# Attention products placed unit by unit instead of slot by slot, and one group of transposes put one slot later

## The reference, cut to what matters

```python
q1, q2 = (q[:, :, :, 0], q[:, :, :, 1])
k1, k2 = (k[:, :, :, 0], k[:, :, :, 1])
attn1 = causal_attn(q1, k1, vcat, scale)
attn2 = causal_attn(q2, k2, vcat, scale)
attn = attn1 - lambda_full * attn2
rms = jnp.sqrt(jnp.mean(attn * attn, axis=-1, keepdims=True) + EPS)
attn = attn / rms * rms_w
attn = attn * (1.0 - LAMBDA_INIT)
x = _layernorm(x + attn.reshape(B, T, H * 2 * HD) @ Wo, axis=-1)
x = _layernorm(x + _L0_ffn_ref(x, router_w, router_b, w1, w2), axis=-1)
```

## Time and profile before

| | us |
|---|---|
| median of 3 runs | 610.83 |
| the runs | 608.61, 611.09, 610.83 |
| span of the profiled execution | 609.5 |
| PE busy | 566.8 |
| DVE busy | 502.4 |
| ACT busy | 427.9 |
| POOL busy | 333.7 |

### The profile page before, as it was taken

One profiled execution on the slowest core, in us unless ns is written; L12 is line 12 of the kernel. 1 busy time (PEld: TensorE's weight loads), 2 busy tenths in 40 slices (PEclk: granted clock), 3 DMA queues, 4 the chain that ended last, 5 costly groups with the idle time before them and its releaser, 6 DMA issues.

```text
span 609.5 us, 30827 instructions
## 1 busy us (share of the span) xinstructions
PE 566.8 (93%) x12925; PEld 339.9 (56%) x12925; DVE 502.4 (82%) x1250; ACT 427.9 (70%) x903; POOL 333.7 (55%) x569
## 2 busy tenths in 40 slices
PE   5499999999999999999999999999999899999992
PEld 1245454555554555455455445545555588899992
DVE  4477898998999899899989989999994878866673
ACT  4004788998888898889888878989789635344441
POOL 5322033773577397737757773943564215765584
PEclk9555799999999999999999999999899999999997
DMA  3603313321331332134123323411102882888510
GB/s 113 182 6 110 100 36 80 108 61 33 100 106 42 96 97 79 50 87 119 35 67 85 109 58 79 112 43 52 51 8 81 275 300 67 274 284 278 189 55 22
DMA packets 44083, 62.85 MB, mean 103 GB/s; under 512 B 13436, under 2 KB 35196, under 8 KB 43800
## 3 DMA queue, kind: packets, MB, share of 16 engines
q1 hardware_dynamic: 38888, 54.31, 30.5%
q0 software_dynamic: 2416, 5.08, 2.3%
q10 hardware_dynamic: 2640, 1.48, 0.9%
HBM read 42.79 MB, written 21.65 MB: 106 GB/s over the span
## 4 chain that ended last, share of the span: by engine, by line
PE 51%; DVE 19%; POOL 15%; issue 6%; DMA 4%; ACT 2%; POOLq 0%; SPq 0%; DVEq 0%; ACTq 0%
DVE mr L1414 14%; PE bank L756 12%; PE bank L689 8%; PE bank L892 7%; PE bank L671 7%; PE bank L907 3%; PE bank L767 3%; POOL x_all L1247 3%; PE bank L773 2%; PE bank L708 2%; PE bank L799 2%; PE bank L809 1%; DMA out_dram<-ynorm,row_u 1%; PE bank L818 1%; POOL out_dram L1306 1%
## 5 line engine op out<-in xcount | busy, mean ns | idle before, releaser
L1414 DVE TENSOR_REDUCE mr<-bank 128x8 f32<-128x512 f32 x576 | 363.4, 681 | 46.1 <-PE bank L689 43.5
L963 ACT ACTIVATE work<-bank 128x512 f32<-128x512 f32 x576 | 313.4, 600 | 56.5 <-PE bank L708 50.4
L756 PE MATMUL bank<-work,v_aug 128*32 128x256 f32 (+6 forms) x2560 | 172.8, 370 | 0.0
L689 PE MATMUL bank<-kd,qd 24*64 24x192 bf16 (+7 forms) x2048 | 172.4, 297 | 0.0
L708 PE MATMUL bank<-qd,kd 27*64 27x320 bf16 (+7 forms) x2048 | 161.5, 288 | 0.0
L671 PEld LDWEIGHTS bank<-bits 32*64 32x64 bf16 x4608 | 79.4, 105 | 142.0 <-DVE mr L1414 65.0
L671 PE MATMUL bank<-bits 32*64 32x64 bf16 (+2 forms) x4608 | 135.2, 213 | 20.3 <-DMA kd<-qk_parts 10.6
L756 PEld LDWEIGHTS bank<-work,v_aug 128*32 128x32 f32 x2560 | 62.4, 110 | 58.4 <-issue 22.6
L1157 POOL CAST msplit<-mt 128x32 bf16<-128x32 f32 x32 | 6.8, 211 | 119.8 <-DVE mt L1424 119.8
L689 PEld LDWEIGHTS bank<-kd,qd 24*64 24x64 bf16 x2048 | 69.4, 112 | 0.0
L708 PEld LDWEIGHTS bank<-qd,kd 27*64 27x64 bf16 x2048 | 65.8, 109 | 0.0
(11 more groups left out here) (204 smaller groups left out, 712.0 us busy)
## 6 DMA issues: line engine op xcount, KB each, us to landing
qk_parts<-parts SPq DMA_DIRECT2D x91, 128.0 KB, 2.7
work<-in_w SPq DMA_DIRECT2D x12, 768.0 KB, 6.4
wbuf<-in_w SPq DMA_DIRECT2D x11, 768.0 KB, 6.7
kd<-qk_parts SPq DMA_DIRECT2D x64, 96.0 KB
qd<-qk_parts SPq DMA_DIRECT2D x62, 96.0 KB
x_sorted<-in_c_pad SPq DMA_DIRECT2D x9, 390.0 KB, 4.5
xr<-x_sorted SPq DMA_DIRECT2D x16, 130.0 KB, 3.4
xt_s<-in_xT SPq DMA_DIRECT2D x8, 256.0 KB
```

Source lines behind the costliest of these rows:

```text
L689: m = pe.matmul(bk[L * c:L * c + L, cols], qd[lo:lo + KROWS, s % 2, second, c, L * n:L * n + L], kd[lo:lo + KROWS, s % 2, second, c, 0:key ...
L756: m = pe.matmul(pv_b[32 * t:32 * t + 32, lo:hi], v_aug[:, vb, kv + v, kb, :], prob[:, pos, r, lo - back:hi - back], start=piece == 0, stop ...
L963: nc.scalar.activation(prob[:, pos, r, :], st_b[no % ST_RING][:, :], ACT.Exp, scale=HD ** -0.5).then_inc(s_sfree, 1)
L1414: V.tensor_reduce(mr[:, s % 2, u % 2, i, i:i + NB], nat_b[no % NAT_RING][:, :].rearrange("p (n t) -> p n t", t=L), AX.X, ALU.max)\
```

## The change

Pieces are keyed by unit instead of slot. Pieces 1, 3, 4, 6 and 8 move one unit earlier, which puts each between the two units of its slot; 0, 2, 5, 7 and 9 stay where they are. Uses stay behind the second unit of a slot. `turn_attn` moves from slot 8 of kind A to slot 0 of kind B, for batches 0 to 5, on PE and on ACT alike (both read `uses`).

```diff
-PV_AT = {3: [0], 5: [1, 2], 6: [3], 7: [4, 5], 8: [6]}
-PV_TAIL_AT = {0: [7], 1: [8, 9]}
+PV_AT = {7: [0], 10: [1], 11: [2], 12: [3], 14: [4], 15: [5], 16: [6]}
+PV_TAIL_AT = {1: [7], 2: [8], 3: [9]}
-CHAIN = {"turn_attn": (8, 8), "wo": (9, 8), "norm": (10, 3), "turn_x1": (10, 8), "router": (11, 2),
+CHAIN = {"turn_attn": (9, 0), "wo": (9, 8), "norm": (10, 3), "turn_x1": (10, 8), "router": (11, 2),
          "chances": (11, 6), "rank": (12, 2), "sort": (12, 6)}
                 for t in range(NC):
                     for u in (2 * t, 2 * t + 1):
                         scores(g, u)
-                    for name, n in uses(g, t):
-                        use(name, n)
-                    if 0 <= g - LAG < NS:
-                        for piece in PV_AT.get(t, []):
-                            pv(g - LAG, piece)
-                    if 0 <= g - LAG - 1 < NS:
-                        for piece in PV_TAIL_AT.get(t, []):
-                            pv(g - LAG - 1, piece)
+                        if u % 2:
+                            for name, n in uses(g, t):
+                                use(name, n)
+                        if 0 <= g - LAG < NS:
+                            for piece in PV_AT.get(u, []):
+                                pv(g - LAG, piece)
+                        if 0 <= g - LAG - 1 < NS:
+                            for piece in PV_TAIL_AT.get(u, []):
+                                pv(g - LAG - 1, piece)
```

## The result

The changed kernel takes 689.5 us (median of 4 runs, 677.1 to 699.9) against 609.7 for the kernel before (608.6 to 611.1): a ratio of 1.115, interval 1.110 to 1.120. It is slower, as forecast, but by 80 us where 21 were forecast, and 41 us above the end of the range. The ratio goes by the two quicker of the four runs, with mean granted clocks of 0.904 and 0.894; the profiled execution, with a span of 694.1 us, is one of the two longer, at 0.876 (the kernel before: 0.950).

The account below looks back on a forecast made before the run. The prediction took PE to set B, and DVE to hold A and D in long stretches. Five whole rounds at +3.0 us (+15) and +6.1 outside them, in all +21 on the median of 610.83, gave 632 us, range 615 to 648.

Parts of the forecast that it names:

- Splitting a pair: On PE, a piece between two units makes them run alone: 0.88 us instead of 0.51, 0.37 more, plus 0.11 per shape change.
- B was forecast at 16.0: Phases of kind B: PE busy from end to end, 13.1 us bare work plus 2.3 plus 0.6, so +2.5 us.
- D at no change: Phases of kind D: PE's new bare work of 12.6 us stays below the 13.02 measured before, so 0.
- The move: turn_attn from A to B: 0.59 us dearer in B, nothing saved in A; already in the forecast, no chance of its own.
- The prediction's own test: What would show it: B near 16 us with PE at no idle time, and DVE idle for over 3 us.
- its signs of being wrong: B staying near 13.5, a unit ahead of a piece taking much under 0.4 us, or A falling below 14.5.
- with PEclk 1.00 throughout: Reading of the earlier trace: the four kinds of phase last 15.43, 13.54, 13.29 and 13.02 us, PE's clock at full speed.
- A, forecast at +0.2: Phases of kind A: DVE sets the pace to 9.5 us, PE then takes 5.8; 0.3 us of lateness comes from D.
- C, forecast at +0.3: Phases of kind C: PE's new bare work 13.5 us against 13.29, with ACT busy for 12.15.
- the lateness of unit 17: In D, piece 6 ahead of unit 17 makes its maxima late by up to 0.78 us; 0.3 taken into A.
- the phases outside the whole rounds: Phases 4, 5, 29, 32 and 33 grow by 1.2, 1.6, 1.3, 1.0 and 1.0 us, the rest 0; sum +6.1.
- DVE's holes: Rival: PE has room and DVE's waits for it, up to 3.9 us a round, close; 603 or 591 us; chance 0.08.

## Why the prediction was right or wrong

**Right: the direction and its cause on PE.** Splitting a pair makes two lone units of 0.43 to 0.44 us out of 0.51 for two, as read from the earlier trace rows, and nothing hides it in B. B was forecast at 16.0 and measured 16.10; D at no change and measured 12.95 against 13.02, though only just: PE is busy for all 12.95 there, where 12.6 was reckoned, and the added products lengthen it by 0.63, as they do B. The move was forecast 0.59 dearer in B, which it is next to the splits. The prediction's own test, B near 16 at no idle time, came out. None of its signs of being wrong came up, for none of them looks at the clock.

**Wrong: "with PEclk 1.00 throughout".** That reading of the earlier trace rows was carried into a kernel whose work is laid out otherwise, and every duration of the sum is one at full clock. The sum has no term for the clock, and neither has any bound or rival. It measured some 47 us of the 85. Splits in the early phases keep it at half until 116.2 us instead of 67.2; splits in D and A besides let it fall in A, in most runs; splits in B and C alone don't; and adding products removes the dips. Only the earlier trace rows of the phases at 1.00 were taken; the three phases at 0.50 ahead of them, visible on the page, should have been asked what let the clock rise.

**Right: A, forecast at +0.2.** It measured +0.33 (15.76 against 15.43). In phase 20 unit 13 starts 9.9 us into the phase and PE takes 5.8 from there, where 9.5 and 5.8 were reckoned. Under the rivals the prediction says that the move saves nothing in A; that doesn't fit with its own 5.8, in which there are no transposes, nor with the runs: with them, in the kernel with the splits alone, A lasts 16.35, 0.59 more.

**Wrong in size: C, forecast at +0.3.** It measured +1.65, eight us over the five rounds. The prediction put the lateness of unit 17 into A alone, behind D (0.3 us). It does its harm in C, behind B, where `wo` and its taker on DVE stand behind that unit; the split at unit 16 alone shows 1.17 of it.

**Undersized: the phases outside the whole rounds.** Phase 5 gained 1.98 (forecast 1.6), phase 29 2.02 (1.3), phases 32 and 33 1.64 and 2.45 (1.0 each); what made them dearer than reckoned wasn't traced. Phases 6 and 7, put at nothing, and A in the first whole round (phase 8) grew by about 1 us each. With C, these and the 8 of the phases with a half clock, PE at full clock comes to the 38 us against 21.

**The rivals.** PE has little room: one split lengthens B by more than half of its price. The Trainium skill ("Perfetto Trace Analysis", section "Identifying the Most-Contended Engine") would have PE's headroom judged by its weight loads, and by the share of its peak arithmetic, which wasn't worked out here. In B of the changed kernel the loads are busy for 7.84 of 16.10 us while PE has no idle time, so for these small products of changing shape the trace doesn't bear the rule of the loads out. The prediction's reading that most of DVE's 3.9 us of waiting lies at the end of A is wrong: the 1.10 of the earlier trace rows is the largest of the eight waits, and the other seven, of 0.21 to 0.60, are spread over the round. DVE's holes didn't close: its waits for PE over phases 20 to 23 grew from 3.9 us in 8 waits to

```profile
DVE mr L1415 <- PE bank L689: 7.4, 21, 0.7
```

The longest is shorter, as the change meant it to be, and there are more of them. The upper end of the range, 648, lies two thirds of the way from 632 to 656, not a third as the prediction says.

## What to carry to other kernels

Ask of every reordering of PE's list which small products run at once before it and no longer after it: two units of 32 rows that start together cost little more than one. Then ask what it does to the granted clock: a sum at full clock has to say why the clock should stay up, and stretches of the old trace at half clock, early and in phase 30 here, are a warning that it may not. Work that is moved to where its engine waits for another (the transposes in the middle of A) shortened its phase, by 0.6 to 0.7 us, and lengthened none of the round; in the whole kernel that gain didn't stand clear of the noise.

## What the runs showed of the hardware

In these stretches PE's busy share doesn't tell when the clock falls. The first stretch below is the beginning of phase 16 in the changed kernel, the clock fell at its end; the second is the same part of phase 16 in the kernel before, where it didn't.

```profile
283.49:290.30 6.81, 6.35 (x191) 2.80 (x184) 6.23 (x15) 5.55 (x11) 6.36 (x11) 1.00 0.22 62
```

```profile
238.65:245.00 6.35, 5.83 (x186) 2.68 (x182) 6.07 (x14) 5.33 (x11) 5.88 (x11) 1.00 0.21 66
```

PE is busy for 93% and 92% of them. And phase 4 of the changed kernel ran for 25.26 us at 0.50 with PE busy throughout, without a rise until its end. The Trainium skill ("TensorE: Matmul & The Clock Gate", section "What's actually happening") says that the gate follows how busy PE has been. By PE's busy share the trace doesn't agree with that, as these figures show. What went with the clock in these runs is which products PE was given: the dips in A came with lone units in D and A, and three products of 128 by 128 weights in every phase, added where PE was mostly busy already, left no dip from 83.3 us to the end of the phases. Which property of a lone unit counts (its 64 columns, its 32 rows, the changes of shape around it) wasn't tried.
